# DLRM tower: upper layers a quarter step earlier, z stored in halves, another order of the last two quarters

## The reference

```python
x = layer_norm(dense_t @ Wd.T, gd, bd)                            # 128 numbers
y = layer_norm(jnp.einsum('bnd,ed->bne', sparse_t, Ws), gs, bs)   # 26 x 128
y = jnp.einsum('bne,pn->bep', y, Wsi)                             # 128 x 32
y = layer_norm(y, gsi, bsi)
T = jnp.concatenate([x[:, None, :], jnp.swapaxes(y, 1, 2)], axis=1)   # 33 x 128
Z = jnp.einsum('bnd,bmd->bnm', T, T)
Zflat = Z[:, TRIL_I, TRIL_J]                                      # 528
z = layer_norm(Zflat @ Wl.T, gl, bl)                              # 512, the first 384 are used
h = jnp.concatenate([z, r_dense_t], axis=1)
h = jnp.maximum(h @ W_top1 + b_top1, 0.0)
h = jnp.maximum(h @ W_top2 + b_top2, 0.0)
y = h @ W_top3
```

## Time and profile before

| | us |
|---|---|
| median of 3 runs | 577.3 |
| lowest, highest | 575.38, 578.61 |
| the profiled execution's own time | 577.42 |
| its span in the profile | 575.6 |
| granted TensorE clock, mean | 0.976 |

### The profile page before, as it was taken

The page is one execution under the profiler, slowest core; times in us unless marked ns, Lnnn a source line. Parts: engine busy times, 40 slices in busy tenths (PEclk is TensorE's granted clock), DMA queues, the critical chain, the costliest instruction groups (busy, mean ns, idle before and its releaser), DMA issues.

```text
span 575.6 us, 18049 instructions
## 1 busy us (share of the span) xinstructions
PE 505.9 (88%) x7271; PEld 378.5 (66%) x7271; DVE 397.2 (69%) x707; ACT 293.6 (51%) x760; POOL 400.8 (70%) x422
## 2 busy tenths in 40 slices
PE   1969779999999898999989998988999899889975
PEld 1844457777776676777666766666676767668664
DVE  4787876777777767777676768766776777767800
ACT  1533565555554555545545646545454645555533
POOL 5777777777777777777777777777777777776000
PEclk9988799999999999899989999998999999999998
DMA  7711311313131312213131312213131211313020
GB/s 259 252 27 30 81 37 27 90 29 90 30 90 29 90 27 70 49 29 91 29 90 27 85 34 68 52 27 89 30 90 30 79 39 39 79 29 87 3 63 1
DMA packets 30999, 35.91 MB, mean 62 GB/s; under 512 B 10588, under 2 KB 19749, under 8 KB 30916
## 3 DMA queue, kind: packets, MB, share of 16 engines
q0 software_dynamic: 13408, 13.81, 12.5%
q1 hardware_dynamic: 17508, 20.94, 11.0%
HBM read 25.54 MB, written 9.18 MB: 60 GB/s over the span
## 4 chain that ended last, share of the span: by engine, by line
POOL 58%; issue 23%; PE 7%; DVE 5%; DMA 5%; ACT 2%; DVEq 0%; ACTq 0%
POOL rows L567 58%; DMA rows<-in_table,ids_based 5%; PE bank_z L700 2%; PE bank_z L633 1%; DVE scaled L397 1%; DVE scaled L372 1%; DVE y L407 1%; PE bank_aw L731 1%; DVE r_vec L433 1%; DVE bank_z L425 1%; ACT y_std L888 1%; PE bank_z L731 1%; PE bank_d L731 0%; DMA ids_based<-in_ids_based 0%; PE bank_z L681 0%
## 5 line engine op out<-in xcount | busy, mean ns | idle before, releaser
L567 POOL DMA_INDIRECT rows<-in_table,ids_based x416 | 399.4, 960 | 129.8 <-issue 122.0
L417 DVE TENSOR_REDUCE y_var<-y_sq 128x32 f32<-128x1024 f32 x63 | 76.9, 1220 | 41.3 <-ACT y_sq L882 41.1
L882 ACT ACTIVATE y_sq<-y 128x512 f32<-128x512 f32 x128 | 80.2, 631 | 34.2 <-DVE y L407 33.6
L433 DVE TENSOR_TENSOR r_vec<-y,bank_z 128x512 f32<-128x512 f32 x128 | 82.3, 684 | 2.4
L666 PE MATMUL bank_b<-mixed,gs_row 64*128 64x512 f32 x128 | 76.9, 682 | 7.8 <-ACT mixed L918 6.1
L681 PEld LDWEIGHTS bank_z<-r_vec 128*32 128x32 f32 x4096 | 46.0, 110 | 56.5 <-issue 54.7
L425 DVE RECIPROCAL bank_z<-y_std 128x32 f32<-128x32 f32 x63 | 22.8, 361 | 84.7 <-ACT y_std L888 84.7
L666 PE MATMUL bank_c<-mixed,gs_row 64*128 64x512 f32 x128 | 76.9, 682 | 0.0
L700 PE MATMUL bank_z<-wl,zd 128*128 128x512 f32 x160 | 75.2, 615 | 0.0
L639 PE MATMUL bank_z<-gram,rows_t 128*128 128x128 f32 x416 | 66.4, 300 | 8.7 <-ACT rows_t L903 8.7
L911 ACT ACTIVATE row_std<-row_var,eps 128x8 f32<-128x8 f32 (+1 forms) x64 | 19.2, 300 | 107.0 <-DVE row_var L381 97.7
(11 more groups left out here) (122 smaller groups left out, 633.8 us busy)
## 6 DMA issues: line engine op xcount, KB each, us to landing
zx<-zs SPq DMA_DIRECT2D x15, 560.0 KB, 3.6
rows<-in_table,ids_based POOLq DMA_INDIRECT x416
dense_t<-in_dense_t SPq DMA_DIRECT2D x1, 2048.0 KB, 9.1
wl<-in_wl SPq DMA_DIRECT2D x1, 1280.0 KB, 12.8
w<-in_w SPq DMA_DIRECT2D x1, 1280.0 KB
zd<-zx SPq DMA_DIRECT2D x15, 80.0 KB
zd<-zx SPq DMA_DIRECT2D x15, 70.0 KB
zd<-zx SPq DMA_DIRECT2D x16, 60.0 KB
```

The costliest lines, as they stand in the source:

```text
L417: v.tensor_reduce(y_var[:, k % BANKS, :], y_sq[:, k % 2, :, :].rearrange("e a (s p) -> e (a s) p", p=PROJ), AX_X, ALU.add).then_inc(y_var_ ...
L433: ins = v.tensor_tensor(r_vec[:, quad:quad + SPB // QUAD, :, Y0:PAD], y[:, k % 2, blk, :].rearrange("e (g s p) -> e g s p", g=SPB // QUAD, ...
L567: nc.gpsimd.indirect_dma_start(rows[t % 2][:, c, D * blk:D * (blk + 1)], None, io["table"], bass.IndirectOffsetOnAxis(ap=ids_all[:, n:n + ...
L882: nc.scalar.activation(y_sq[:, k % 2, blk, :], y[:, k % 2, blk, :], ACT.Square).then_inc(y_squared, 1)
```

## The change

**The body.** The upper part moves: the first quarter of tile T has now `third_layer(T-2)` and `first_dense(T-1)`, the second `linear(T-1)`, the third `turn_z(T-1)` (ahead of `interact`) and `first_layer(T-1)`, the fourth `second_layer(T-1)`. ACT and DVE follow: `linear_root`, `linear_reciprocal`, `scale_z` and `keep_turned_z` stand in the third quarter, with `keep_turned_z` ahead of `row_root` and `keep_z`. The PSUM banks of the layers, and some waits for them, change with it. The four sums of x are taken one per tile. The z of each tile is stored in two halves, the first when two quarters are kept.

**The end.** The y chain of quarter 62 runs by blocks too, its reciprocals and those of quarter 63 go to a tile in SBUF (`y_r_last`) and no longer wait for `zs_kept`. The order of PE, DVE and ACT in the last steps is another.

```diff
-Z_OUT = 1 * 16
+Z_OUT = 2 * 16
...
+        y_r_last = sb("y_r_last", [P, 2, 2 * SPB])
...
-        bank_lin = [bank_l] * (TILES - 2) + [bank_t] * 2
-        bank_h1 = [bank_d] * (TILES - 2) + [bank_l, bank_m]
-        bank_h2 = [bank_d] * (TILES - 1) + [bank_b]
-        bank_o = [bank_d] * (TILES - 1) + [bank_c]
+        bank_s = [bank_d[:], bank_l, bank_l, bank_l]
+        bank_lin = [bank_l] * (TILES - 1) + [bank_t]
+        bank_h1 = [bank_d] * (TILES - 1) + [bank_m]
+        bank_h2 = [bank_d] * (TILES - 2) + [bank_b] * 2
+        bank_o = [bank_l] * (TILES - 1) + [bank_c]
...
+            def y_reciprocal_block(n, blk):
+                k = QUARTERS - 2 + n
+                dve.wait_ge(y_std_done, k + n + blk + 1)
                 part = slice(blk * SPB, (blk + 1) * SPB)
-                v.reciprocal(y_r[:, part], y_std[:, k % BANKS, part]).then_inc(y_r_done, 1)
+                v.reciprocal(y_r_last[:, n, part], y_std[:, k % BANKS, part]).then_inc(y_r_done, 1)
...
+            def y_scale_block(n, blk):
+                k = QUARTERS - 2 + n
...
+                    y_r_last[:, n, blk * SPB:(blk + 1) * SPB].rearrange("e (g s o) -> e g s o", s=QUAD, o=1)
+                    .broadcast_to([P, SPB // QUAD, QUAD, PROJ]), ALU.mult)
+                if blk:
+                    ins.then_inc(r_ready, 1)
...
-                if old:
+                if w >= 1:
                     y_mean_square(w - 1)
                     y_reciprocal(w - 1)
                     y_scale(w - 1, 0)
                     y_scale(w - 1, 1)
-                if q == 3 and 1 <= tile < TILES - 1:
+                if q == 2 and 1 <= tile < TILES - 1:
                     linear_reciprocal(tile - 1)
-                if ahead:
-                    square_form(w + 1)
-                    row_mean_square(w + 1)
-                if new:
+                if w == QUARTERS - 2:
                     keep_y(w, 0)
-                if ahead:
-                    row_reciprocal(w + 1)
-                    scale_rows(w + 1)
-                if new:
-                    keep_y(w, 1)
+                square_form(w + 1)
+                row_mean_square(w + 1)
+                if w < QUARTERS - 2:
+                    keep_y(w, 0)
+                row_reciprocal(w + 1)
+                scale_rows(w + 1)
+                keep_y(w, 1)
...
-            end = QUARTERS - 1
-            y_mean_square_block(end, 0)
-            y_mean_square_block(end, 1)
-            for blk in range(2):
-                y_reciprocal_block(end, blk)
-                dve.wait_ge(y_r_done, end + blk + 1)
-                y_scale(end, blk)
+            for n in range(2):
+                if n == 1:
+                    keep_y(QUARTERS - 1, 0)
+                    keep_y(QUARTERS - 1, 1)
+                y_mean_square_block(n, 0)
+                y_mean_square_block(n, 1)
+                for blk in range(2):
+                    y_reciprocal_block(n, blk)
+                    y_scale_block(n, blk)
...
             for t in range(TILES - 1):
-                sp.wait_ge(zs_kept, BANKS * (t + 1))
                 if t:
                     sp.wait_ge(z_moved, Z_MOVES * t)
-                sp.dma_start(zx.rearrange("j p k g i -> (j p) k g i"), zs[:]).then_inc(z_out, 16)
+                for first, end in ((0, 2 * ZQUADS), (2 * ZQUADS, QUADS)):
+                    sp.wait_ge(zs_kept, BANKS * t + end // ZQUADS)
+                    sp.dma_start(zx.rearrange("j p k g i -> (j p) k g i")[:, :, first:end, :], zs[:, :, first:end, :])\
+                        .then_inc(z_out, 16)
                 sp.wait_ge(z_out, Z_OUT * (t + 1))
...
                         pe.wait_ge(z_moved_last, 16 * 2)
                     pe.wait_ge(sumx_placed, t + 1)
-                    if t == TILES - 2:
+                    if t == TILES - 1:
                         pe.wait_ge(quad_done, QUARTERS)
                     if t:
                         pe.wait_ge(z_kept, t)
+                        pe.wait_ge(out_kept, min(t, TILES - 2))
...
-                    first_layer(tile - 2, range(4))
-                if q == 1 and tile >= 2:
-                    second_layer(tile - 2)
-                if q == 2:
-                    if tile >= 2:
-                        third_layer(tile - 2)
-                    if tile >= 1:
-                        linear(tile - 1, range(STEPS))
+                    third_layer(tile - 2)
+                if q == 0 and tile >= 1:
+                    first_dense(tile - 1)
+                if q == 1 and tile >= 1:
+                    linear(tile - 1, range(STEPS))
+                if q == 2 and tile >= 1:
+                    first_layer(tile - 1, range(4))
                 if q == 3 and tile >= 1:
-                    first_dense(tile - 1)
-                    turn_z(tile - 1)
+                    second_layer(tile - 1)
...
+                if w >= BANKS and w % BANKS == 2:
+                    turn_z(w // BANKS - 1)
                 if old:
                     interact(w - 1)
-                if 3 <= w < 7:
-                    add_up_x(w - 3)
+                if w in (3, 7, 11, 15):
+                    add_up_x(w // BANKS)
```

115 lines of the change are left out of this document (59 added, 56 removed).

## The result

| | before | after |
|---|---|---|
| median us (4 runs each) | 577.95 | 606.46 |
| lowest, highest | 575.38, 579.66 | 604.88, 607.89 |
| profiled execution, its span | 577.42, 575.6 | 607.89, 606.1 |
| granted clock, mean | 0.976 | 0.961 |

The ratio is 1.050 with the interval 1.0469 to 1.0531. The forecast of 576.9 was 29.6 us too low, and the top of its range (574.2 to 579.3) 27.2 us. Of the cases of the prediction only one is of the right kind, "the body is no longer hidden"; it had been priced at up to 1 us, "and more if it grows from tile to tile", with a chance of 0.06.

What follows compares the result with a forecast made beforehand. POOL's gathers were taken to bound the kernel up to 528.7 us, so only the end could move: -0.3 + 0.9 - 1.25, rounded to -0.4, took 577.42 to 577.0, and the runs' median 0.1 lower gave 576.9; range 574.2 to 579.3.

Steps and rivals of the forecast that it cites:

- the body is no longer hidden: Rival: in the body, keep_turned_z or linear holds quarter 61; up to +1 us, more if it grows by tile; chance 0.06.
- What bounds the kernel now: Up to the last gather at 528.71 the time is POOL's; only the end, 528.7 to 575.6, can move.
- Part 1: Body: upper layers a quarter earlier; longest loop some 8.5 us, hidden by 10 us of gathers; cost 0, at most 1 us.
- Part 2: z store in halves: a half lands in 3.2 us; PE may stand 0.4 us at linear(14); worth 0.
- Part 3: Head start at quarter 62: turn(62) goes when its rows are there, about 524.4; gain 1.3 us.
- Part 4: From y_root(61): row_root(63) behind keep_z(61), at 537.5, loses most of the head start; -0.3 us of the 1.3 stays.
- Part 5: Last quarter: turn_z(14) now ahead of interact(63), which comes at 548.45; +0.9 us on keep_z(63) and first_layer(14).
- Part 6: End: linear(15) ahead of third_layer(14), following second_layer(14) at 556.8 without waiting for z; -1.25 us.
- Sum: Whole kernel: -0.3 + 0.9 - 1.25, rounded to -0.4 us by the starts of linear(15).
- The clock: PE in the end: first_layer(15) ran at low clock, 1.6 us; one low stretch was assumed in both kernels.
- the clock falls in the new thin stretch: Rival: low clock after 545.4 to 551.3 slows first_layer(14); +1.6 us, 578.5, or 579.6 with second_layer(14); chance 0.16.
- second rival: The low clock in the end's new thin stretch, slowing first_layer(14): 578.5 us, or 579.6; chance 0.16.

Runs made afterwards that it cites:

- a_no_z_wait: Changed kernel, but the z moves of tiles 0 to 14 go to an unread tile and linear does not wait for them; 580.13 us, ratio 1.0028.
- b_end_2: Kernel before with linear(15) ahead of third_layer(14), linear_root(15) ahead of keep_out(14), and first_dense(14) moved behind turn_z(14); 575.06 us, ratio 0.9974.
- b_end_1: Kernel before with linear(15) ahead of third_layer(14) on PE and linear_root(15) ahead of keep_out(14) on ACT; 575.17 us, ratio 0.9953.
- a_row_root_first: Changed kernel with ACT's three z_t copies (keep_turned_z) behind row_root in a tile's third quarter; 598.41 us, ratio 1.0335.
- a_dense_ahead: Changed kernel with first_dense(tile - 1) moved from quarter 0 to quarter 1, directly ahead of linear; 603.29 us, ratio 1.0446.
- b_half_store: Kernel before with the z of each tile stored in two halves; 578.28 us, ratio 0.9992.

## Why the prediction was wrong, point by point

a_no_z_wait is the changed kernel with the body under its cover. Its end shows what the forecast's parts 3 to 6 were worth on their own terms:

```profile
524.50 0.49 PE L654 MATMUL bank_z<-ident,rows 128*128 128x128 f32 x3
...
537.10 0.30 ACT L931 ACTIVATE row_std<-row_var,eps 128x6 f32<-128x6 f32 x1
...
547.43 0.55 PE L727 MATMUL bank_z<-ident,z_row 128*128 128x128 f32 x3 [2.54 <-ACT z_row L976]
...
550.79 5.49 PE L749 MATMUL bank_d<-z_t,w 128*128 128x128 f32 x24 [2.11 <-ACT z_t L983]
...
558.68 4.56 PE L720 MATMUL bank_z<-wl,zd 128*128 128x512 f32 x10
```

- **What bounds the kernel now.** Right for the kernel before: the gathers set the pace up to 528.7. The mistake is the sentence drawn from it, that what an edit does before that is worth nothing unless PE is late at the end. It was true only up to some 2 us a tile (29.6 over the tiles), and I did not work that figure out, though the 29.6 us that PE waited for rows stood in the list of waits.
- **Part 1, the step that failed.** "So POOL hides it; the body costs 0." I compared one loop, estimated at 8.5 us, with the 10 us of one quarter's 8 gathers. The loop came out at 9.11 us, which alone would have been no harm. But the gathers run ahead over several quarters, so what has to be compared is the sum of a tile's four loops with 26 gathers: 34.2 against 32.9. And the longer loop was not the worse one: that with `linear` went to 10.83. "If that cover failed, at most 1 us" priced one quarter and not fifteen tiles; the body's loss was 28 us. Once the body is late nothing gives the time back, for the loss comes again in each tile.
- **Part 2.** The halves are worth 0, as forecast, and a half landed in about 3.3 us (3.2 forecast). The 0.4 us that `linear` "may stand there" is the same number that broke part 1: taken at the last tile, called harmless because rows came later there, and never carried to the other fourteen. It measured between 0.66 and 3.02 us, 21.6 in all.
- **Part 3.** Right under cover: `turn(62)` at 524.50 in a_no_z_wait, 524.38 in b_end_2, forecast 524.4. In the changed kernel itself that head start has no meaning, since PE comes to all quarters late.
- **Part 4.** Right: `row_root(63)` stood directly behind `keep_z(61)`, at 537.10 (forecast 537.5), and in the changed kernel, 29 us later, in the same way (below).
- **Part 5.** Right in kind: `turn_z(14)` ran before `interact(63)`, at 547.43, and `interact(63)` at 547.91, where 548.45 was forecast for it; the last y scaling had ended at 546.69 (forecast 547.1).
- **Part 6.** Right in kind: `linear(15)` followed `second_layer(14)` without a wait for z. It was 1.9 us later than forecast, and the slow `first_layer(14)` (5.49 instead of 2.94 us) costs 2.55, more than all of it. In b_end_1, which has this part alone, the kernel was 0.5% faster (0.3 to 0.65).
- **Sum.** As written, -0.3 + 0.9 - 1.25 is -0.65 and not -0.4. The 0.9 already holds the 0.3, so 0.9 - 1.25 is what the -0.4 stands for. This slip is 0.3 us at most and not what failed.
- **The clock.** The rival "the clock falls in the new thin stretch" happened, in the changed kernel and in a_no_z_wait alike. Its 2.55 us cover the 2 us that the end lost. I should have given it more than 0.16, for the row that spoke for it came from a stretch as thin.

Timeline of the changed kernel's end, with the window over the start of `first_layer(14)`:

```profile
566.27 0.30 ACT L932 ACTIVATE row_std<-row_var,eps 128x6 f32<-128x6 f32 x1
...
579.94 5.49 PE L750 MATMUL bank_d<-z_t,w 128*128 128x128 f32 x24 [2.11 <-ACT z_t L984]
...
587.84 4.56 PE L721 MATMUL bank_z<-wl,zd 128*128 128x512 f32 x10
...
596.12 4.51 PE L750 MATMUL bank_aw<-z_t,w 128*128 128x128 f32 x24 [1.25 <-ACT z_t L984]
```

```profile
580.00:582.00 2.00, 2.00 (x9) 2.00 (x10) 0.00 (x0) 0.00 (x0) 0.83 (x2) 0.50 0.19 34
```

These rows answer to the earlier trace rows. From `linear(15)` to the end of the span it is 606.1 - 587.84 = 18.3 us, before 575.6 - 557.20 = 18.4. With the body hidden the forecast would have been 578.5 by its second rival, and a_no_z_wait took 580.1. So the end was read well but for the clock, and all but some 3 of the 29.6 us is the body.

**How the loss adds up.** a_no_z_wait is 0.3% from the kernel before, within what can be measured, so the loss hangs on the wait for z. Waiting (21.6) and the slow clock (87.5 - 77.4 = 10.1) put 31.7 us into the loops of pass 1, and the reciprocal of quarter 61 comes 28.9 us later than in a_no_z_wait (562.3 against 533.4). Nearly all of it arrives, since even a_no_z_wait has little cover: its loops sum to 31.7 us where the old order had 30.5. `linear` made pass 1 longer (6.93 to 8.28), and pass 2, which it left, did not get shorter (8.90 to 9.11), as `linear_root`, `turn_z`, `keep_turned_z` and `first_layer` now follow one another in it. At quarter 12 a_no_z_wait was already 6.5 us behind the kernel before (141.8 to 135.2). With 1.2 us of cover per tile instead of 2.3 it needed the whole body to make up for that, and met the gathers only near the end.

**What stays open.** Why the moves started 1 us later in six of the tiles. Why a_row_root_first has a median 8 us lower while its loops in the profile are the same. The runs show only that it is not the wait for `row_r` by itself, since with the wait for z gone the same edit is worth nothing (603.29 and 603.95). That `linear` falls to the low clock in fewer tiles in its faster executions would fit and was not shown; in the slow one that was profiled it was busy 84.7 us. Nor was it tried to split `linear`'s steps over two passes, or to bring the z store forward.

## What to carry to other kernels

When a queue of transfers bounds a pipeline, its cover is one number: its time per tile less the sum of the tile's own loops. Work it out before calling any edit in the body free (here some 2 us, from the waits for rows or from a kernel with the transfers left out), and hold an added wait against it times the number of tiles, with the slow matmuls behind the wait. A consumer pulled nearer to its producer needs the whole round trip in between (here 7.25 us of store, issue and landing against 6.18); and work moved into the hole only helps if the loop that it leaves gets shorter.

## What the hardware showed that was not expected

- After a wait of PE for a DMA of only 1 to 3 us the following matmuls can run at the low clock: the ten records of `linear` took 7.39 us after 3.02 us of waiting (granted clock 0.62 from 252 to 260), 4.67 after 1.07. Over the kernel that was 87.5 us against 74.7 in a_dense_ahead, where PE waited 1.7 us in all.
- One useless matmul ahead of such a wait made the kernel 6 to 8 us faster (606.46 to 598.71, by the ratios 1.050 to 1.039).
- The split store behaved as the whole one: in b_half_store the moves started 2.89 us after the second half, in the kernel before also 2.89 us after the whole (423.22 to 426.11), though the halves went out in rows of 320 bytes. Over tiles 1 to 14 it was 2.89 to 4.55 us with halves and 2.78 to 3.98 with the whole.
- The level of the clock at the same place of the program differed between kernels that differ a little elsewhere: `first_layer(14)` took 2.94 us in the kernel before and in b_end_2 and 4.57 in b_end_1, `first_layer(15)` the other way round in before and b_end_1. That is 1.6 us each, as much as the edits of the end. No kernel was profiled twice, so whether one and the same kernel changes is not shown.
